# Linear attention and FFN in one kernel: masked states in the running sum, one product for a block's chunk sums, and a later norm and transposition of the next input

## The reference, cut to what matters

```
x  = x + LinAttn(layernorm(x))
y  = layernorm(x)
x  = x + y + 0.5 * (silu((layernorm(y)*gamma + beta) @ W1 + b1) @ W2 + b2)      # FFN, 256 -> 1024 -> 256
LinAttn, 16 heads of 16:  q = elu(x Wq)+1,  k = elu(x Wk)+1,  v = x Wv
  out_i = sum_{j<=i} (q_i . k_j) v_j / sum_{j<=i} (q_i . k_j)        # causal
```

## Time and profile before

| | |
|---|---|
| median of 3 runs | 1490.65 us (1488.85 to 1491.71) |
| the profiled execution: its own time, its span | 1494.15 us, 1492.1 us |
| busy, share of the span | TensorE 95%, VectorE 83%, ScalarE 69%, GpSimd 53% |
| instructions | 64840, of which TensorE 27482 matmuls |
| mean granted clock of TensorE | 0.98 of 2.4 GHz |
| DMA | 72.13 MB moved, mean 48 GB/s |

### The profile page before, as it was taken

One profiled execution on the slowest core, in us unless ns is written; L12 is line 12 of the kernel. 1 busy time (PEld: TensorE's weight loads), 2 busy tenths in 40 slices (PEclk: granted clock), 3 DMA queues, 4 the chain that ended last, 5 costly groups with the idle time before them and its releaser, 6 DMA issues.

```text
span 1492.1 us, 64840 instructions
## 1 busy us (share of the span) xinstructions
PE 1414.1 (95%) x27482; PEld 1231.5 (83%) x27482; DVE 1233.3 (83%) x2077; ACT 1036.8 (69%) x1789; POOL 793.0 (53%) x469
## 2 busy tenths in 40 slices
PE   7669999999999999999999999999999999999978
PEld 7558888888888888888888888888888888888857
DVE  5678888888889888888988888988888898888774
ACT  4357777766777876777776677787677778667643
POOL 2124566545566645456654556664545665455443
PEclk8779999999999999999999999999999999999989
DMA  5111011111101111101111110111110111111010
GB/s 155 38 44 57 25 38 50 56 56 56 52 16 47 54 56 56 56 28 35 50 56 56 56 50 18 47 54 56 56 56 28 35 49 56 56 56 39 11 41 29
DMA packets 83299, 72.13 MB, mean 48 GB/s; under 512 B 14912, under 2 KB 82752, under 8 KB 83264
## 3 DMA queue, kind: packets, MB, share of 16 engines
q1 hardware_dynamic: 81904, 71.62, 15.6%
q10 hardware_dynamic: 1360, 0.01, 0.1%
HBM read 38.03 MB, written 16.78 MB: 37 GB/s over the span
## 4 chain that ended last, share of the span: by engine, by line
PE 78%; DVE 11%; issue 7%; ACT 2%; POOL 1%; DMA 0%; DVEq 0%; ACTq 0%; POOLq 0%
PE sc L287 24%; PE ring L287 18%; PE num L287 6%; DVE state L644 5%; PE sc L408 5%; DVE probs L627 4%; PE sc L353 4%; PE sc L354 3%; PE num L455 2%; PE ring L353 2%; PE ring L394 2%; PE num L335 2%; PE ring L427 2%; ACT silu_f L832 2%; PE ring L354 1%
## 5 line engine op out<-in xcount | busy, mean ns | idle before, releaser
L982 POOL TENSOR_TENSOR s_lo<-silu_f,s_hi 128x512 fp32r<-128x512 f32 x256 | 416.1, 1631 | 565.4 <-ACT s_hi L847 562.2
L840 ACT ACTIVATE silu_f<-silu_f 128x512 f32<-128x512 f32 x256 | 156.4, 622 | 77.1 <-DVE silu_f L617 76.2
L627 DVE TENSOR_TENSOR probs<-sc,causal 128x1024 f32<-128x1024 f32 x128 | 150.8, 1220 | 31.3 <-PE sc L408 31.2
L888 ACT ACTIVATE hn<-x,hn_add,ln_rstd 128x256 f32<-128x256 f32 x128 | 66.5, 591 | 152.9 <-DVE hn_add L736 152.9
L832 ACT ACTIVATE silu_f<-sc,bias,scale 128x512 f32<-128x512 f32 x155 | 120.1, 776 | 63.8 <-PE sc L354 63.6
L847 ACT ACTIVATE s_hi<-silu_f 128x512 fp32r<-128x512 f32 x256 | 158.7, 621 | 1.1
L644 DVE TENSOR_TENSOR state<-kv_sums,head_ones 128x896 f32<-128x896 f32 x64 | 144.5, 2303 | 0.0
L287 PE MATMUL sc<-w_hi,s_hi 128*128 128x256 f32 x496 | 142.8, 288 | 0.0
L353 PE MATMUL sc<-gt_hi,w_q 128*128 128x512 f32 x286 | 122.8, 429 | 21.1 <-DVE probs L627 21.1
L287 PE MATMUL ring<-w_hi,s_lo 128*128 128x256 f32 x496 | 139.9, 282 | 0.0
L287 PE MATMUL ring<-w_hi,s_hi 128*128 128x256 f32 x496 | 139.9, 282 | 0.0
(11 more groups left out here) (186 smaller groups left out, 4270.0 us busy)
## 6 DMA issues: line engine op xcount, KB each, us to landing
x_in<-in_x SPq DMA_DIRECT2D x32, 512.0 KB, 4.0
rb<-den_rows SPq DMA_DIRECT2D x512, 32.0 KB, 1.9
xb<-in_x SPq DMA_DIRECT2D x32, 512.0 KB, 4.7
out<-out_t SPq DMA_DIRECT2D x64, 256.0 KB, 2.4
probs<-in_q SPq DMA_DIRECT2D x2, 512.0 KB, 8.4
silu_f<-in_q SPq DMA_DIRECT2D x2, 512.0 KB, 6.4
res<-in_sc SPq DMA_DIRECT2D x1, 512.0 KB, 6.8
out_t<-in_sc SPq DMA_DIRECT2D x1, 512.0 KB, 9.3
```

The source lines that it names most:

```text
L627: masked.done(e.tensor_tensor(probs[:, t, 2 * h:2 * h + 2, :, :, :].rearrange("p g m a q -> p (g m a) q"), sc[:, 2 * h:2 * h + 2, :].rearr ...
L840: silu.done(e.activation(slot, slot, ACT.Silu))
L982: sl.done(e.tensor_tensor(s_lo[:, j, :], silu_f[:, j % SLOTS, :], s_hi[:, j, :].bitcast(F32), ALU.subtract))
```

## The change

The scan on VectorE now sums and masks in one instruction: (sum + chunk) times `state_keep`, which is zero for the rows of the other head of a pair and at the end of a row of chunks. The result, 512 elements per partition, is the state that `from_states` reads, each pair of heads on its own 32 rows; the snapshots and `head_ones`' spreading are gone. For that, `v_pad` has a copy with zeros for each half of a block, and one product over all 128 rows gives both halves' chunk sums. The denominators of a block of 128 tokens come out in 32 rows, so the reciprocal covers 128 columns, and SyncE copies in 8 DMAs. The norm of the next input moves from the end of an iteration to the middle, its transposes behind `from_states`; all orders and the banks are written anew, and `free_bank` issues its waits in another order. Cut to its core:

```diff
-            "ht0": (1,), "ht1": (0,), "kt0": (7,), "kt1": (6,), "sc0": (2, 3, 4, 5), "f0a": (7,), "f0b": (1,),
-            "xt0": (6,), "xt1": (0,), "f1a": (2,), "f1b": (7,), "f2a": (3,), "f2b": (1,), "kv": (6,),
-            "sc1": (2, 3, 4, 5), "f3a": (1,), "f3b": (7,), "f4a": (4,), "f4b": (5,), "num": (0, 1),
-            "f5a": (2,), "f5b": (4,), "f6a": (6,), "f6b": (5,), "f7a": (3,), "f7b": (4,),
-            "k0": (7,), "q0": (2,), "k1": (6,), "q1": (0,), "v0": (5,), "v1": (4,), "wo0": (3,), "wo1": (1,),
-            "z0": (7,), "den": (3,), "z1": (5,),
+            "ht0": (6,), "ht1": (0,), "kt0": (1,), "kt1": (7,), "sc0": (2, 3, 4, 5), "f0a": (1,), "f0b": (0,), "kv": (6,),
+            "f1a": (7,), "f1b": (1,), "sc1": (2, 3, 4, 5), "f2a": (7,), "f2b": (6,), "num": (0, 1), "f3a": (5,),
+            "f3b": (7,), "f4a": (4,), "f4b": (2,), "f5a": (5,), "f5b": (6,), "xt0": (5,), "xt1": (7,), "f6a": (3,),
+            "f6b": (2,), "f7a": (6,), "f7b": (4,), "k0": (7,), "q0": (0,), "k1": (6,), "q1": (4,), "v0": (2,), "v1": (5,),
+            "wo0": (3,), "wo1": (1,), "z0": (0,), "den": (7,), "z1": (3,),
...
-            def chunk_states(r):
+            def chunk_states():
 
                 w.need(kt_sb, 0)
                 w.need(v_sb, 0)
-                if r == 0:
-                    free_bank(w, "kv", present)
-                else:
-
-                    w.need(half_pe, 0)
-                w.hold()
-                toks = slice(HALF * r, HALF * (r + 1))
+                free_bank(w, "kv", present)
                 for t in range(T):
                     for m in range(C):
                         for g in range(PAIRS):
-                            last = e.matmul(kv_bank[PW * g:PW * (g + 1), t, :, 2 * m + r],
-                                            k_tok[toks, m, t * P + PW * g:t * P + PW * (g + 1)],
-                                            v_pad[toks, m, t * PAIRS + g, 0:4:3, :],
+                            last = e.matmul(kv_bank[PW * g:PW * (g + 1), t, :, 2 * m:2 * m + 2].rearrange("p x r -> p r x"),
+                                            k_tok[:, m, t * P + PW * g:t * P + PW * (g + 1)],
+                                            v_pad[:, :, m, t * PAIRS + g, 0:4:3, :],
                                             start=True, stop=True, skip_group_check=True)
-                (half_pe, upd_pe)[r].done(last)
+                upd_pe.done(last)
...
                             for g in range(PAIRS):
                                 last = e.matmul(num[PW * g:PW * (g + 1), r, num_of(r, t, m)],
-                                                v_pad[toks, m, t * PAIRS + g, 2 * odd:2 * odd + 2, :],
+                                                v_pad[toks, r, m, t * PAIRS + g, 2 * odd:2 * odd + 2, :],
                                                 probs[toks, t, g, m, odd, :],
                                                 start=(t == 0 and m == 0 and odd == 0), stop=(odd == 1), skip_group_check=True)
                 av_pe.done(last)
 
             def from_states(t):
-                w.need(snap, 0, t)
+
+                w.need(summed, 0)
+                w.hold()
                 for c in range(1, 2 * C):
                     m, r = divmod(c, 2)
                     for g in range(PAIRS):
-                        last = e.matmul(num[PW * g:PW * (g + 1), r, num_of(r, t, m)],
-                                        state[:, t, c - 1, PW * g:PW * (g + 1)], phi_q[:, t, chunk(r, m)],
+                        pair = slice(PW * g, PW * (g + 1))
+                        last = e.matmul(num[pair, r, num_of(r, t, m)],
+                                        state_view[pair, t, c - 1, :], phi_q[pair, t, chunk(r, m)],
                                         start=False, stop=False, skip_group_check=True)
...
                 for t in range(T):
-                    for half in range(2):
-                        g = 2 * t + half
-                        last = e.matmul(use_bank("den")[32 * g:32 * g + 32, 0:2 * P], head_one[:, :],
-                                        qk[:, t, 2 * P * half:2 * P * (half + 1)], start=True, stop=True,
+                    for m in range(C):
+                        last = e.matmul(use_bank("den")[32 * m:32 * m + 32, 0:P], head_one[:, t, :, :, :],
+                                        qk[:, t, m * P:(m + 1) * P], start=(t == 0), stop=(t == T - 1),
                                         skip_group_check=True)
...
             fc1(0)
+            chunk_states()
+            fc1(1)
+            scores(1)
+            fc1(2)
+            values(0)
+            fc1(3)
+            fc1(4)
+            values(1)
+            fc1(5)
+            from_states(0)
+            from_states(1)
             x_transposes(0)
             x_transposes(1)
-            fc1(1)
-            fc1(2)
-            chunk_states(0)
-            scores(1)
-            chunk_states(1)
-            fc1(3)
-            fc1(4)
-            values(0)
-            fc1(5)
-            values(1)
-            from_states(0)
-            from_states(1)
             fc1(6)
             fc1(7)
...
             def sum_states():
+
                 if not A:
                     return
                 w.need(upd_pe, 0)
-                kv_sb.done(e.tensor_tensor_scan(kv_sums[:, :], scan_keep[:, :], use_bank("kv"), 0.0, ALU.mult, ALU.add))
-
-            def snapshots(t):
-                if not A:
-                    return
-                w.need(kv_sb, 0)
                 w.need(num_pe, -1)
-                shape = [P, STATES, PAIRS, PW]
-                snap.done(e.tensor_tensor(
-                    state[:, t, :, :].rearrange("p n (g x) -> p n g x", x=PW),
-                    kv_view[:, t, 0:STATES, :][:, :, None, :].to_broadcast(shape),
-                    head_ones[:, :].rearrange("p (g x) -> p g x", x=PW)[:, None, :, :].to_broadcast(shape), ALU.mult))
+                summed.done(e.tensor_tensor_scan(state[:, :], use_bank("kv"), state_keep[:, :], 0.0, ALU.add, ALU.mult))
...
             mask(0, 0)
             mask(0, 1)
             ffn_sum(0)
-            input_lo(0)
+            sum_states()
             ffn_sum(1)
-            input_lo(1)
+            mask(1, 1)
+            mask(1, 0)
             ffn_sum(2)
-            mask(1, 0)
-            mask(1, 1)
-            sum_states()
+            if N:
+                ve_x_hat(e, w, 1)
             ffn_sum(3)
-            snapshots(0)
-            snapshots(1)
             ffn_sum(4)
             ffn_sum(5)
             attention(0)
+            input_lo(0)
+            input_lo(1)
             attention(1)
             ffn_sum(6)
+            attention_lo(0)
             ffn_sum(7)
             if preparation[3]:
                 preparation[3]()
-            attention_lo(0)
+            residual()
+            attention_lo(1)
             if N2:
                 ve_norm_x(e, w, 2)
-            residual()
-            attention_lo(1)
             features(0)
             cumulate(0)
             features(1)
@@ -809,11 +808,9 @@
             norm_x1()
             reciprocals()
             norm_factors()
-            final(0)
             if preparation[1]:
                 preparation[1](1)
-            if N2:
-                ve_x_hat(e, w, 2)
+            final(0)
             if N:
                 final(1)
...
-                for h in range(2):
+                for r in range(2):
+                    toks = slice(HALF * r, HALF * (r + 1))
                     last = e.activation(
-                        v_pad[:, 2 * n + h, :, 0:4:3, :],
-                        use_bank(f"v{n}")[:, h * D:(h + 1) * D].rearrange("p (r a x) -> p r a x", a=2, x=HD),
-                        ACT.Copy)
+                        v_pad[toks, r, 2 * n:2 * n + 2, :, 0:4:3, :].rearrange("p c g a x -> p (c g) a x"),
+                        use_bank(f"v{n}")[toks, :].rearrange("p (c a x) -> p c a x", a=2, x=HD), ACT.Copy)
                 v_sb.done(last)
...
             ffn_input_hi(0)
             ffn_input_hi(1)
             keys_out(0)
             keys_out(1)
             ffn_scaled(0)
-            input_hi(0)
-            input_hi(1)
             ffn_scaled(1)
             ffn_scaled(2)
             ffn_silu(0)
+            ffn_silu(1)
             ffn_hi(0)
-            ffn_silu(1)
-            ffn_silu(2)
             ffn_hi(1)
             ffn_scaled(3)
+            ffn_silu(2)
             ffn_scaled(4)
             ffn_hi(2)
             ffn_silu(3)
             ffn_scaled(5)
+            ffn_silu(4)
             ffn_hi(3)
-            ffn_silu(4)
+            ffn_hi(4)
+            input_hi(0)
+            input_hi(1)
             ffn_silu(5)
             ffn_scaled(6)
-            ffn_hi(4)
+            attention_hi(0)
+            ffn_hi(5)
             ffn_scaled(7)
-            attention_hi(0)
             ffn_silu(6)
-            ffn_hi(5)
+            attention_hi(1)
             ffn_silu(7)
             ffn_hi(6)
-            if N:
```

(53 more changed lines are left out.)

157 lines of the change are left out of this document (84 added, 73 removed).

## The result

The changed kernel takes **1650.57 us** (median of 4 runs, 1645.82 to 1655.49) against 1491.18 for the kernel before beside it (4 runs, 1488.85 to 1493.53): 1.1069 times as long, 95% interval 1.1032 to 1.1106. The forecast was 1453, range 1430 to 1476. It is slower by 159 us, and 198 away from the forecast. None of the rivals names what happened, though one of them, the serialized row tiles, gave a time close to it (1624).

What follows compares the result with a forecast made beforehand. TensorE, 95% busy, was taken as the bound, with idle time in attention and the FFN's first layer. Terms -0.97 - 0.35 - 0.12 + 0.24 = -1.2 us a batch, over 31 batches -37 us, gave 1453 us, range 1430 to 1476.

Steps and rivals of the forecast that it cites:

- the serialized row tiles: Rival: in from_states, row tiles writing one bank run one after another; +4.3 us a batch, 1624 us; 5%.
- Parts 1 to 4: TensorE per batch: mask stall -0.97, chunk states -0.35, from_states -0.12, blocks of another shape +0.24; sum -1.2 us.
- Part 6: Input norm and transposes moved later: projections released at 2.6 us, TensorE arrives at 2.85; hidden, 0.2 us to spare.
- Part 5: Snapshots gone from VectorE: 4.54 us that only from_states waits for; no further gain on TensorE's path.
- part 3: from_states: same 112 instructions on 32 rows instead of 128; gain 0.12 us a batch, the wait for its snapshot.
- What a batch costs is what TensorE issues plus what it waits for in that stage.: Premise for attention and the FFN's first layer, 20.8 us of a 44.18 us batch: sum made by starts on TensorE's timeline.
- GpSimd as the bound: Rival: last ffn_lo, now behind the residual's bias addition, holds up fc2(0); +0.7 us a batch, 1513 us; 4%.
- A new wait before the projections: Rival: one late ScalarE copy shows ahead of the projections; gain only 0.6 us a batch, 1472 us; 20%.

Runs made afterwards that it cites:

- e5: Changed kernel with 100 idle increments ahead of TensorE's first instruction, and x_hat and the residual back where they stood before the change: 1456.47 us, 0.9745 of before.
- e1: Changed kernel with 100 idle semaphore increments ahead of TensorE's first instruction, shifting where its loop starts: 1551.74 us, 1.0391 of before.
- e8: e5 without the 100 increments, so the loop starts where it does in the changed kernel: 1622.73 us, 1.0881 of before.
- e12: e8 with 76 idle increments right ahead of TensorE's loop, where it waits for hn anyway: 1446.61 us, 0.9679 of before.
- e9: Changed kernel with 40 idle increments ahead of TensorE's first instruction: 1712.85 us, 1.1465 of before.
- e10: Changed kernel with 300 idle increments ahead of TensorE's first instruction: 1769.14 us, 1.1842 of before.
- e2: Kernel before the change with 100 idle increments ahead of TensorE's first instruction, nothing in its loop touched: 1713.49 us, 1.1475 of before.

## Why the prediction was wrong

It was wrong in two of its steps, and e5 shows that the rest of the sum was right to 0.2 us a batch. e5's TensorE, by the chain of waits and then by its timeline, and last the timeline's row of the kernel before:

```profile
695.30 0.44 PE ring L340 x4
...
738.02 0.44 PE ring L340 x4
```
```profile
695.14 0.60 PE L340 MATMUL ring<-ident,hn 128*128 128x128 f32 x4
...
699.24 1.10 PE L429 MATMUL ring<-v_pad,k_tok 128*32 128x64 f32 x64
700.27 0.50 PE L358 MATMUL ring<-gt_hi,w_q 128*128 128x512 f32 x1
...
709.68 1.95 PE L460 MATMUL num<-phi_q,state 32*32 32x64 f32 x112
711.56 0.66 PE L331 MATMUL sc<-ident,x_hat 128*128 128x128 f32 x4
...
714.35 0.40 PE L292 MATMUL ring<-xt_hi,wk_hi 128*128 128x512 f32 x1
```
```profile
662.67 1.03 PE L335 MATMUL num<-ident,hn 128*128 128x128 f32 x8
```

- *Parts 1 to 4, the sum of -1.2 us.* Right in its mechanisms, 0.2 too small. The period is 42.72 us (43.0 foretold). From `ffn_in` to the projections it is 19.21 us by the timeline, against 20.61 before (662.67 to 683.28): -1.40. Which part holds the 0.2 stays open. No idle time at `fc1(4)`; chunk states 1.03 us (1.05 foretold); `from_states` 1.88 (1.85), with no wait. e5 has 11.7 us of increments at its start, so 1456.47 stands for about 1445, 8 us better than the forecast.
- *Part 6, the chain behind the transposes.* Right in size: first transpose to first projection 2.79 us (2.85 foretold). Wrong in its first sentence, and this is the first step that failed: "`x_hat` moves between masks and sums" was given no price. I moved it with its 1.37 us from beside an idle GpSimd to beside `s_lo`, where it takes 4.30; and the residual, whose order on both engines changes, went unpriced altogether: 3.65 instead of 1.38. Together 5.2 us of VectorE a batch, more than the 4.54 that part 5 took off. In e1 TensorE shows it as three waits, 43.2 us for `phi_q`, 18.7 ahead of `x_transposes` and 14.4 for `xt_lo`, 76.3 of the 95.3 us between e1 and e5; in e5's loop all three are gone.
- *Part 5.* "On TensorE's path that is part 3 and no more": no engine's load was added up anew. VectorE's busy time would have shown it, 1233.3 us before and 1236.0 in e1 without any snapshot.
- *"What a batch costs is what TensorE issues plus what it waits for in that stage."* The second step that failed, and the dearer one. It takes for granted that instructions are there when their turn comes. The change shortens TensorE's loop and nonetheless makes it touch one piece more; 98.8 us of the loss (e1), or 166.3 where VectorE isn't late (e8 to e5); both are what is left after the increments' own 9.0 and 11.7 us at the start, and e12, where most of them fall into a wait, is 176.1 below e8. The page of before had the row to ask about, 27 packets on the instruction queue in a run of 32 batches: the loop stayed on the chip. I didn't ask whether it still would.
- *Rivals.* Row tiles of one bank: the 44 and 68 instructions ran at 22 and 19 ns, and e5's 112, in the same tiles, at 16.8, below the 27 from which that rival decides; its 1624 was near the result by chance. By the rule of the Trainium skill, "TensorEngine Tiling (Array Packing)", Gotcha 1: PSUM Pressure, they would have been serialized; for four row tiles that write four partition groups of one bank these runs show no such cost. GpSimd as the bound: its `s_lo` wait at `fc2(0)` didn't come, but that rival's own evidence, 5.12 us for a pair of `s_lo` beside the snapshots, looks like this contention seen from GpSimd's side: without the snapshots the mean of `s_lo` falls from 1631 ns to 1386 in e1. I used it to make GpSimd faster and never asked what VectorE pays. A new wait before the projections: there in e1 (14.4 us in 30), but because VectorE came late to `xt_lo`, not ScalarE to its copies.

## What to carry to other kernels

Read the instruction queue's packets first whenever a change alters how many instructions an engine has, ahead of the loop as well as in it: packets of one run through the program mean that the loop stays on the chip, a multiple of the loop's turns means that it is fetched again, and some dozens of idle instructions ahead of the loop, enough to bring it across a border, tell in one run what that costs; too few or too many, as in e9 and e10, make it worse. The duration of an operation on VectorE depends on what GpSimd does beside it, so one that is moved doesn't keep the duration of its old row. In these traces operations with an input from PSUM kept theirs, and so did the statistics; `x_hat`, the residual and `gt_lo`, with all inputs in SBUF, didn't. And undo two suspects together as well as one by one: here one of them showed 28 us alone and 95 once the other was gone.

## What the runs showed that I had not expected

- A kernel's time can hang on where its loop begins: 1494 us or 1713 for the same loop (e2), by 100 instructions that do nothing. Where all of the loop fits, no piece is fetched twice (26 packets for the 6,758 instructions of e1, so about 260 a packet); where it touches one piece more, all are: 9 packets a turn for 8 pieces, not one.
- A packet takes 1.02 us on its queue, but in the busy part of a batch they mostly followed one another at 3.3 to 4 us, while TensorE runs through the 256 instructions of `values` in 1.42 us. So the attention stage is starved and the projections, some 350 instructions in 23.36 us, are not. What holds the packets 3.3 us apart wasn't tried. The Trainium skill, "Runtime: NRT & Kernel Launch", Instruction fetch mechanics, gives blocks of 16 KiB with 256 instructions and 2,048 instructions for TensorE, which are 8 blocks; a loop of 7 pieces, with the one behind it, would fill them, and one of 8 with a ninth, as the nine packets a turn suggest, would be one too many. The runs agree with that reading and don't prove it. That a crossing is "mostly hidden" doesn't hold here: a turn of nine packets costs 3.5 to 5.9 us (98.8 and 166.3 over 28).
- The same number of packets costs 62 us more or less by where the borders fall: behind two long waits in a row the granted clock stood at 0.50 (e9), in the changed kernel, where a first wait of 1.67 us is followed by one of 0.69, it stayed at 1.00.
